# Folding a causal mask into unused contraction rows, moving elementwise work between engines, and a new hand-written order in a decoder layer

## The reference

```python
x1 = x  + min_gru(rmsnorm(x))             # gates g, v, d; h_t = a_t h_(t-1) + x_t
x2 = x1 + Wo(attention(rmsnorm(x1)))      # 16 heads of 8, causal: key k <= query q
x3 = x2 + Wout(silu(Wgate n) * (Wup n))   # n = rmsnorm(x2), hidden width 512
y1 = layernorm(x + x3)
s  = (y1 Wq)(ctx Wk)^T / sqrt(128) + mask # cross attention on a context
y2 = layernorm(y1 + softmax(s) (ctx Wv^T + bv))
c  = top-2 of softmax(y2 Wr) over 8 experts
out = layernorm(y2 + sum_e c_e * y2 (Wi[e] Wmo[e]))
```

## Time and profile before

| | us |
|---|---|
| median of 3 runs | 284.08 (283.85 to 284.08) |
| profiled execution, time | 282.77 |
| its span, first to last instruction | 281.0 |
| TensorE busy | 246.2 |
| VectorE busy | 207.0 |
| ScalarE busy | 164.0 |
| GpSimd busy | 117.9 |

### The profile page before, as it was taken

One profiled execution on the slowest core, in us unless ns is written; L12 is line 12 of the kernel. 1 busy time (PEld: TensorE's weight loads), 2 busy tenths in 40 slices (PEclk: granted clock), 3 DMA queues, 4 the chain that ended last, 5 costly groups with the idle time before them and its releaser, 6 DMA issues.

```text
span 281.0 us, 7859 instructions
## 1 busy us (share of the span) xinstructions
PE 246.2 (88%) x2222; PEld 188.3 (67%) x2222; DVE 207.0 (74%) x785; ACT 164.0 (58%) x598; POOL 117.9 (42%) x332
## 2 busy tenths in 40 slices
PE   2958579699989999999999999999999999997752
PEld 1746464577868787878787878778777767574320
DVE  5413324364779898989889898989897979778765
ACT  3526526658585859585858585858575555554210
POOL 6321322435453455454646464635353442423321
PEclk9986959999999999999999999999999999999877
DMA  4993131333141223432322234232323230000000
GB/s 125 261 213 85 40 86 41 90 88 99 35 101 36 73 66 71 114 73 71 72 71 65 69 85 107 50 88 51 87 50 87 49 99 0 15 0 12 12 9 20
DMA packets 33707, 20.12 MB, mean 72 GB/s; under 512 B 20480, under 2 KB 31232, under 8 KB 33664
## 3 DMA queue, kind: packets, MB, share of 16 engines
q1 hardware_dynamic: 33232, 19.48, 27.7%
q10 hardware_dynamic: 432, 0.13, 0.2%
HBM read 14.16 MB, written 5.24 MB: 69 GB/s over the span
## 4 chain that ended last, share of the span: by engine, by line
PE 64%; SPq 10%; DMA 7%; DVE 7%; issue 4%; POOL 4%; ACT 2%; POOLq 0%; DVEq 0%; ACTq 0%
PE ps L620 10%; PE ps L688 9%; PE ps_scores L558 6%; PE ps_probs L575 6%; PE ps L509 5%; DMA q_stack<-nmT 5%; SPq L282 5%; PE ps_probs L577 5%; PE ps_scores L560 5%; DVE neg_max L1029 3%; SPq L338 3%; PE ps L521 3%; PE ps L587 2%; PE ps L538 2%; SPq L337 2%
## 5 line engine op out<-in xcount | busy, mean ns | idle before, releaser
L1029 DVE TENSOR_REDUCE neg_max<-ps_scores 128x4 f32<-128x512 f32 x64 | 44.0, 688 | 17.7 <-PE ps_scores L560 14.1
L839 ACT ACTIVATE probs<-ps_probs 128x512 f32<-128x512 f32 x64 | 38.4, 600 | 20.8 <-PE ps_probs L577 20.4
L383 POOL TENSOR_SCALAR ve<-mv 128x1 f32<-128x1 f32 x48 | 9.4, 196 | 69.9 <-DVE mv L1110 37.1
L688 PE MATMUL ps<-w_moe,y2T 128*128 128x512 f32 x64 | 35.2, 636 | 0.0
L620 PE MATMUL ps<-xT,guT 128*128 128x128 f32 x256 | 34.0, 276 | 0.2
L620 PEld LDWEIGHTS ps<-xT,guT 128*128 128x128 f32 x256 | 32.2, 191 | 2.0 <-issue 0.3
L575 PEld LDWEIGHTS ps_probs<-q_stack,k_stack 75*128 75x128 bf16 x256 | 19.1, 98 | 13.7 <-ACT probs L839 5.3
L1162 DVE SCALAR_TENSOR_TENSOR acc<-ps,moe_c,acc 128x128 f32<-128x128 f32 x96 | 27.7, 344 | 0.5
L385 POOL TENSOR_TENSOR lrs<-ve,neghalf 128x1 f32<-128x1 f32 x48 | 26.3, 549 | 4.0
L385 POOL TENSOR_TENSOR rs<-ms,neghalf 128x1 f32<-128x1 f32 x48 | 26.3, 549 | 4.0
L575 PE MATMUL ps_probs<-q_stack,k_stack 75*128 75x128 bf16 x256 | 25.2, 221 | 3.1 <-DMA q_stack<-nmT 2.4
(11 more groups left out here) (154 smaller groups left out, 609.9 us busy)
## 6 DMA issues: line engine op xcount, KB each, us to landing
q_stack<-qk_scratch SPq DMA_DIRECT2D x48, 96.0 KB
k_stack<-qk_scratch SPq DMA_DIRECT2D x48, 96.0 KB
qk_scratch<-qk_parts SPq DMA_DIRECT2D x16, 192.0 KB, 2.3
ctx_sb<-in_ctx_dram SPq DMA_DIRECT2D x4, 256.0 KB, 3.5
qk_scratch<-qk_parts SPq DMA_DIRECT2D x16, 64.0 KB, 2.2
out_dram<-out_sb SPq DMA_DIRECT2D x16, 64.0 KB, 1.8
x_all<-in_x_dram SPq DMA_DIRECT2D x1, 640.0 KB, 8.2
raw<-in_L_ffn_Wi_dram SPq DMA_DIRECT2D x1, 512.0 KB, 5.2
```

What stands on the lines that cost most here:

```text
L688: nc.tensor.matmul(as_one(view(fill)), y2T[:, b, :], w_moe[:, 4 * n:4 * n + 4, :], start=True, stop=True).then_inc(S[("moe_m0_ps", "moe_m1 ...
L839: nc.scalar.activation(probs[:, n, :, :], ps_probs[:], ACT.Exp, scale=HD ** -0.5).then_inc(S["att_p"], 1)
L1029: nc.vector.tensor_reduce(neg_max[:, b, QUARTER * n:QUARTER * n + QUARTER], ps_scores[:], AX_X, ALU.max, negate=True).then_inc(S["max_max" ...
```

## The change

- `SROWS` goes from 75 to 125. Rows 72 to 124 of both stacks hold constant patterns: for query m < 53, row 72 + m has -1e30 at column m on the query side and 1 at every column beyond m on the key side. The mask of queries 0 to 52 so comes out of the four matmuls. The mask matmuls shrink to the columns that are left: 4 x 74 in `scores`, 4 x 75 in `scores_turned`. The maxima use rows 125 to 127. VectorE fills the stacks once from two GpSimd patterns, in four copies.
- The three `layernorm_apply` go to GpSimd.
- Expert terms 0 to 3 are scaled by ScalarE (four instructions) and added by GpSimd (two); VectorE keeps terms 4 to 7.
- Cross scores are kept negative (weights and mask negated once), which leaves out a small negation for each tile; choosing the top two takes one small instruction less.
- The GRU runs two tiles a step from the start (ends in steps 8 to 10), the context two tiles a step from step 3 (ends in steps 11 and 12). The later pieces have larger lags: FFN 8 and 9, cross attention 10, experts 11 and 12. Every list has a new order, and banks are assigned anew.
- The SP queue loads weights in another order, with a semaphore for each, and the stores stand between `parts_stack` and `max_stack`.

```diff
-SROWS = QROWS + PARTS
+SROWS = P - PARTS
+MROWS = SROWS - QROWS
-MAX_LAG = 10
+MAX_LAG = 12
...
+        def pair(t, lag, turn, piece, *more):
+            k = 2 * (t - lag) + turn
+            if 0 <= k < TILES:
+                piece(k, k % 2, *more)
...
-                nc.tensor.matmul(ps_scores[:], identb[:], above[:], start=False, stop=True)
+                nc.tensor.matmul(ps_scores[:, :, MROWS + 1:P], identb[:], above[:, :, MROWS + 1:P], start=False, stop=True)
...
-                nc.tensor.matmul(ps_probs[:], identb[:], below[:], start=False, stop=True)
+                nc.tensor.matmul(ps_probs[:, :, MROWS:P], identb[:], below[:, :, MROWS:P], start=False, stop=True)
...
+            def mask_rows(b):
+                dve.wait_ge(S["mask_rows"], 3)
+                nc.vector.tensor_copy(q_stack[:, b, :, :], rows_q[:].unsqueeze(1).to_broadcast([P, HEADS, P]))
+                nc.vector.tensor_copy(k_stack[:, b, :, :], rows_k[:].unsqueeze(1).to_broadcast([P, HEADS, P]))
...
+            def layernorm_apply(n, k, b, src, dst, rsd, done):
+                nc.gpsimd.tensor_scalar(dst, src, mv[:, n, b, 0:1], lrs[:, n, b:b + 1], ALU.subtract, ALU.mult)
...
+            def moe_scale(k, b):
+                for e in range(4):
+                    last = nc.scalar.activation(terms[:, b, e, :], view("moe_experts_0")[:, e, :], ACT.Copy, scale=moe_c[:, b, e:e + 1])
...
+            def moe_add(k, b):
+                nc.gpsimd.tensor_tensor(term_pairs[:, b, :, :], terms[:, b, 0:2, :], terms[:, b, 2:4, :], ALU.add)
+                nc.gpsimd.tensor_tensor(first_half[:, b, :], term_pairs[:, b, 0, :], term_pairs[:, b, 1, :], ALU.add)
...
+            def moe_mix(k, b):
+                term(4, 0, y2[:, b, :], "moe_acc")
+                after(dve, "moe_first", k + 1)
+                term(5, 1, first_half[:, b, :], "moe_acc")
+                term(6, 0, acc[:, b, 0, :], "moe_acc")
+                term(7, 1, acc[:, b, 1, :], "moe_high")
...
 # TensorE's list after, one step (pieces that run once left out)
+  att_values 0 (6), gru_turn_back (pair), max_turn (5), att_values 1, 2 (6), gru_turn_back (pair), gru_gates (pair),
+  moe_experts 0 (12), xat_turn (10), att_values 3 (6), ffn_up (9), ffn_turn (8), ctx_project, gru_turn, ctx_turn (pair),
+  xat_scores (10), scores 0 (4), scores_turned 0 (5), v_project (4), att_project (7), att_back (6), scores 1,
+  scores_turned 1, ctx_project (pair), moe_experts 1 (12), ctx_turn (pair), qkv_turn (2), moe_turn (11), scores 2,
+  scores_turned 2, ffn_down (9), gru_gates (pair), scores 3, moe_logits (11), scores_turned 3, att_turn (6),
+  xat_turn_probs (10), qk_project (2), gru_turn (pair), ffn_gate (8), xat_values (10)
 # VectorE: maxima 1, ..., maxima 2, moe_mix, maxima 3, ..., maxima 0; GpSimd: gru_power, gru_decay, ffn_power, max_split, ...
```

More of the change, by code:

```diff
@@ L47 @@
 CTX_LOAD = 4
-MAX_LAG = 10
[L53 to L78, removed]
-]
-BANK = {piece: n for n, users in enumerate(USERS) for piece, _, _ in users}
+MAX_LAG = 12
+BANKS = [
+    [("att_back", "att_o"),
+     ("att_turn", "att_oT"),
+     ("att_values", "att_vT")],
+    [("gru_turn_back", "gru_x1"),
+     ("xat_turn", "xat_xT"),
+     ("ctx_project", "ctx_kv"),
+     ("v_project", "max_v"),
+     ("moe_experts_1", "moe_high"),
+     ("xat_values", "xat_z")],
+    [("gru_gates", "gru_tanh"),
+     ("ffn_up", "ffn_h"),
+     ("moe_turn", "moe_xT"),
+     ("xat_turn_probs", "xat_pT")],
+    [("max_turn", "max_mT"),
+     ("ffn_turn", "ffn_xT"),
+     ("qkv_turn", "qkv_xT"),
+     ("ffn_down", "ffn_z")],
+    [("moe_experts_0", "moe_terms"),
+     ("ctx_turn", "ctx_T"),
+     ("att_project", "att_x2"),
+     ("moe_logits", "moe_lg"),
+     ("qk_project", "qkv_rest")],
+    [("gru_turn", "gru_xT"),
+     ("xat_scores", "xat_sm"),
+     ("ffn_gate", "ffn_t1")],
+]
+BANK = {fill: n for n, fills in enumerate(BANKS) for fill, _ in fills}
+READER = {fill: done for fills in BANKS for fill, done in fills}
 ALU = mybir.AluOpType
@@ L229, in decoder_layer @@
         moe_c = sb("moe_c", [P, 2, EXPERTS])
+        terms = sb("terms", [P, 2, 4, P])
+        term_pairs = sb("term_pairs", [P, 2, 2, P])
+        first_half = sb("first_half", [P, 2, P])
         acc = sb("acc", [P, 2, 2, P])
@@ L258, in steps @@
             for t in range(LAST):
[L259 to L271, removed]
+                step(t)
+        held = {}
         def bank_free(eng, k, fill):
-            after(eng, *last_use(k, fill))
+            bank = BANK[fill]
+            if bank in held:
+                after(eng, *held[bank])
+            held[bank] = READER[fill], k + 1
         block = stack.enter_context(nc.Block())
@@ L304, in _, with load_gate @@
[L304 to L313, removed]
+            def load_gate():
+                load(raw[:, R_GATE:R_GATE + FF, :], Wgate.rearrange("(n p) k -> p n k", p=P), "w_in_g")
@@ L375, in _ @@
[L375 to L378 removed]
+            pool.wait_ge(S["const_pool"], 3)
+            nc.gpsimd.tensor_copy(identb[:], ident[:]).then_inc(S["const_pool"], 1)
+            nc.gpsimd.memset(flat[:, 0, :], 0.0).then_inc(S["const_pool"], 1)
```

538 lines of the change are left out of this document (301 added, 237 removed).

## The result

| | before | after |
|---|---|---|
| time, median | 284.08 us | 269.47 us (267.92 to 269.99) |
| ratio to before | | 0.9459, 95% interval 0.9395 to 0.9522 |
| profiled execution, time and span | 282.77, 281.0 | 269.52, 267.8 |
| A, to the first scores | 30.84 | 27.61 |
| B, to quarter 0 of the transposed scores of tile 0 | 11.40 | 11.49 |

The forecast was 263.7 with a range of 256 to 272. The measured time lies in that range, but above the stretch of 256 to 268 that was given 0.60, and inside the 268 to 273 of the first rival. The sum of the four parts came out near because errors cancel: C is 8.9 us shorter than forecast (177.0), A 3.4 shorter (31.0), D 17.6 longer (43).

A forecast was written before the change was run, and what follows sets the result against it. TensorE's columns were taken to bound the middle steps, with the maxima's loop close behind. Parts 31.0 + 10.9 + 177.0 + 43 made 261.9 us, 263.7 with 1.77 outside the span; range 256 to 272.

The forecast's parts named there:

- A: Filling, up to TensorE's first scores: left at 31.0 us (28 to 34), against 30.84 before.
- B: First loop alone, from first scores to tile 0's transposed quarter 0: 10.9 us, against 11.40 before.
- first rival: Whole kernel: only the narrower mask columns pay, the new order nets nothing; 271 us (268 to 273), chance 0.20.
- C: Fifteen steps between transposed quarter 0 of tile 0 and of tile 15: 177.0 us, 23.8 less than before.
- D: From tile 15's transposed quarter 0 to the end: 43 us (38 to 48), against 37.92 before.
- The mask: TensorE's mask matmuls: 0.09 us less each, eight a tile, 0.74 a step, 11.8 us over 16 tiles.
- The 11.4: Fill steps 5 to 11: loop through the maxima's DMA sets them, 11.4 us each (10.4 to 12.2).
- Step 12: The step with the last context product: 12.5 us.
- the 0.6 added for waits: Steps 13 to 19: 0.6 us of waits added to TensorE's 11.5, giving 12.1 each, seven times.
- Busy times: Engines' totals: VectorE down by 40 us, ScalarE up by some 20, GpSimd up by some 35.
- Only the columns: Whole kernel: the new order wins nothing in the fifteen steps that the end doesn't take back; 271 us, chance 0.20.
- The other three rivals: Expert mix holds the maxima, 273 to 282, 0.08; low clock, 285 and more, 0.04; better still, under 256, 0.08.

The follow-up runs named there:

- e7: The kernel before with the mask part alone (125 contraction rows, narrower mask matmuls, row patterns), order and norms as before: 276.47 us, ratio 0.9718.
- e4: The changed kernel with all eight expert terms on VectorE, terms 0 to 3 ahead of maxima 0: 274.57 us, ratio 0.9641.
- e1: The changed kernel with all three norm steps on VectorE instead of GpSimd, for all tiles: 290.05 us, ratio 1.0184.
- e5: The changed kernel with only the experts' norm step on VectorE, behind maxima 3, for all tiles: 268.19 us, ratio 0.9439.
- e8: The changed kernel with the experts' norm step (behind maxima 3) and the FFN's and cross attention's residual adds on VectorE: 268.99 us, ratio 0.9457.
- e12: The changed kernel with experts' norm step (behind cross attention's moments) and two residual adds on VectorE, store one step later, six GpSimd test steps: 267.36 us.
- e3: The changed kernel with mask matmuls of 512 columns again, the 125 contraction rows kept: 277.93 us, ratio 0.9760.

## Why the prediction was right, and where it was not

**A** (forecast 31.0, measured 27.6). The sum took the earlier context load and the separate semaphores at nothing. In all runs based on the changed kernel A is 26.95 to 28.1, in e7, with the old order and the new row patterns, 31.7. So the patterns and their copies, put at nothing, cost some 0.9 there, and the rest of the change gains about 4. Which piece of it does was not tried.

**B** (10.9, 11.5): 0.6 off. The loss that was forecast, 0.5, is not there in this execution. In the runs that share its first steps B is 10.4 to 11.2, and 10.7 in e7.

**The mask** (11.8, measured 8.0 to 8.5). The mechanism and the 0.09 us were right. The size was off because the sum gave all of it to the step, and the step gained 0.5 in the old order, with the gap seen in e7, and 0.6 in the new (medians 12.12 and 11.53), not 0.74. Why 0.1 is missing in the new order, where TensorE has no idle time, stays open.

**C** (177.0, measured 168.1). The changed kernel is bound by TensorE's columns from step 11 on (102.62 us of 103.31 between 103.85 and 207.16), as forecast for 12 and later. In the six steps before, it is busy 59.73 of 64.75 us. Its longest waits there are for a DMA, but not for the one that the forecast named: quarter 0 of the scores waits for the reads that fill the stacks with the parts, not for the DMA of the maxima:

```profile
49.25 0.38 PE L647 MATMUL ps_scores<-k_stack,q_stack 125*128 125x128 bf16 x4 [0.66 <-DMA q_stack<-qk_scratch]
```

Three such waits make 1.8 us between 39.10 and 103.85, the DMA of the maxima none. The additions on top of the bounds were too large. The seven fill steps took 76.3 instead of 79.8, 10.9 on average: the first four 10.1 to 10.8, near the 10.0 to 10.4 summed for the loop, the last two 11.5, TensorE's bound. The 11.4 came from a step with another order. Step 12 took 11.4 instead of 12.5, and the last seven 80.3 instead of 84.7: 11.5 was the bound from the earlier trace rows, and nothing of the 0.6 added for waits came. The edits that the sum priced at nothing in C are cover, and it is thin: by e4 four terms put back on VectorE cost 4.9 us of C; by e1 three norm steps cost 17.4, both with these places in the list.

What C lost is for the most part TensorE's work, not its waits. Before and after:

```profile
42.24:243.08 200.84, 194.01 (x1941) 151.69 (x1940) 163.82 (x620) 134.62 (x491) 92.75 (x263) 1.00 0.28 70
39.10:207.16 168.06, 162.34 (x1797) 132.69 (x1795) 120.81 (x404) 122.98 (x455) 107.75 (x262) 1.00 0.33 80
```

Idle time went from 6.8 to 5.7 us, busy time down by 31.7. C has 144 of TensorE's instructions less and D 109 more (148 and 257), at 18.4 us more of busy time (25.4 and 43.8, a part of it from the low clock). Most of the rest are the columns.

**D** (43, measured 60.6). This is the step that failed: each of tile 15's pieces "can now stand behind a neighbour's (0.1 to 0.9, mean 0.35): +4". The sum looked for a bound in TensorE's work (28 us) and in tile 15's own chain, and priced the larger lags per piece. But a tile goes through the drain one step at a time, and it has seven steps to go instead of three. Each costs what holds the lists longest there, TensorE's list in the first full step, then GpSimd's or a ring between two lists, 7.6 us on average after and 9.8 before. Four more steps at 7.6, less 3 x 2.2 on the others, is 23.8; less 1.5 for an earlier first mix and with 0.3 at the end, it is the 22.7 us that D grew. GpSimd's 0.80 us per norm step is a part of it, but a small one: at 0.31 a step would have 1.5 us less of GpSimd, and e5 (0.8 less), e8 and e12 (1.7 less) show what then holds: in the third to fifth step of the drain rings at 7.3 to 8.0, and D at 58.8 to 60.8. So the mis-sized term is the number of steps, not the norm step. That number is counted in the two traces; no run here changes a lag alone. Nor was the low clock of the last 22 us in the sum. That D "is past 50" had been named as what would make the forecast wrong; C's surplus paid for half of it, and A's for a fifth: that the time is in the range is luck as far as D goes.

**Busy times.** GpSimd's excess of 23.5 is the norm step, as counted above. VectorE lost 13 us less than forecast. A part of that: four terms in a row take 1.13 us, 0.28 each and not 0.34, and the copies that fill the stacks take 3.2 us where a memset of 1.8 stood. Why ScalarE gained 11.3 us, when its new instructions alone sum to 18.3, was not taken apart.

**The rivals.** Only the columns, given 0.20, is what happened, with other sizes. It said that the new order wins nothing in C that D doesn't take back, and 271 us. By e3, with wide masks still in place, C is 23.9 us shorter than before (200.8 to 177.0), and D takes 22.9 of that back (60.8). What is left over are the columns (8.6 from e3 to the changed kernel, 8.0 by e7, not 11.8) and an earlier start (3.4), which the rival did not have. So the part of the forecast on which the 263.7 rested, that the order wins much more in C than it loses in D, did not come: forecast 12.7 in C (23.8 less 15 x 0.74) against 5.1 in D, measured 23.9 against 22.9. The other three rivals did not come. What a measurement can tell is more than the 0.6 us of the prediction: the interval of the ratio is 1.8 us to either side.

## What to carry to other kernels

Count a larger lag in steps: where the last pieces of a tile are moved back by a step of lag, one whole step is added to the drain, at the pace of the fullest in-order list or of the slowest ring between two lists there (four steps at 7.6 us here), and only what it takes off the saturated steps pays for that. Work that leaves the saturated steps for the drain is not saved: here 109 of TensorE's instructions moved there, and D grew by 22.7. Two lists in strict order can hold each other by places alone. When work moves to another engine, name what stands behind the instruction that now waits and follow it once round, the DMA queue too, since a store that waits for a late result holds every transfer behind it.

Price a moved instruction by its operation and its operands, not by its shape alone.

## What the runs showed of the hardware

The price of one GpSimd instruction of the same shape (128x128 float32, two operations in one) depends on the operations and on where the scalars come from. In e12, in GpSimd's timeline, three of the six steps (multiply and add with constants, the same with per-row operands, subtract and multiply with constants); the others repeat them:

```profile
82.69 0.30 POOL L502 TENSOR_SCALAR form<-ident 128x128 f32<-128x128 f32 x1
93.99 0.45 POOL L502 TENSOR_SCALAR form<-ident,neghalf 128x128 f32<-128x128 f32 x1
105.23 0.65 POOL L502 TENSOR_SCALAR form<-ident 128x128 f32<-128x128 f32 x1
```

The pair subtract and multiply costs 0.35 us more than the pair multiply and add, per-row operands cost 0.15, and both together make the 0.80 of the norm step; on VectorE the step took 0.34 in e8. The 0.30 is also, within 0.01, what `gru_decay` (L408 before) takes, a multiply and an add with constants, from which the prediction had its price. Whether it is the subtract or the order of the two operations that costs was not tried; among instructions with two tensors a subtract is not dearer than an add (128x256: 0.67, written as bfloat16, and 0.73 in the changed kernel).

The Trainium skill ("GPSIMD Engine Reference", section 3.1, "Elementwise — side-by-side cycle accounting") gives a measured 2.6 cycles an element, and for an add of two tensors. By it, as an estimate with the 1.2 GHz that the Trainium skill states in "Trainium Architecture — The Big Picture", "The five engines, in one table", 128 more elements a row take 0.28 us. The trace agrees for such adds: 128x256 takes 0.27 more than 128x128 (0.73 and 0.46, L509 and L512). It is no figure for the norm step, which has one tensor as input and takes 0.80.

By these rows, as an estimate, a norm step written as a multiply and an add with per-row operands would take 0.45, with one more small instruction for the product of mean and scale (0.19 us for one of 128x1). No run here has it.
